# A two-layer attention kernel on one core: one step more between scores, weighing and product, and another order on each queue

## What is computed

```
def gat_layer(x, W, adj):
    Wh, Ws = split(x @ W, 2, axis=-1)
    a = softmax(Wh @ Ws.T, axis=-1) * adj
    return leaky_relu(a @ Wh + x, 0.01)
y = gat_layer(gat_layer(x, W[0], adj), W[1], adj)
out = layernorm(x + y)
```

## Time and profile before

| | us |
|---|---|
| median of 3 runs | 1668.36 |
| the profiled execution | 1670.49 |
| its span, first to last instruction | 1668.1 |
| TensorE matmul busy | 1591.5 (95%) |
| VectorE busy | 1231.2 (74%) |
| GpSimd busy | 872.0 (52%) |
| ScalarE busy | 679.5 (41%) |

### The profile page before, as it was taken

One profiled execution on the slowest core, in us unless ns is written; L12 is line 12 of the kernel. 1 busy time (PEld: TensorE's weight loads), 2 busy tenths in 40 slices (PEclk: granted clock), 3 DMA queues, 4 the chain that ended last, 5 costly groups with the idle time before them and its releaser, 6 DMA issues.

```text
span 1668.1 us, 23318 instructions
## 1 busy us (share of the span) xinstructions
PE 1591.5 (95%) x8104; PEld 1321.9 (79%) x8104; DVE 1231.2 (74%) x1558; ACT 679.5 (41%) x1175; POOL 872.0 (52%) x807
## 2 busy tenths in 40 slices
PE   7899999999999999999889999999999999999996
PEld 6788888887888888887677878887888888888884
DVE  4677777777777777677636787787887888787885
ACT  4434444444444444444333444444434443444442
POOL 0155555555555555555512556555555556555565
PEclk9999999999999999999899999999999999999998
DMA  5267777777667777877915677776778777777774
GB/s 183 81 176 186 190 189 187 185 192 190 185 184 193 184 182 180 206 186 215 249 34 131 176 193 190 192 196 190 179 190 208 191 184 190 196 191 191 195 196 123
DMA packets 167748, 302.57 MB, mean 181 GB/s; under 512 B 39760, under 2 KB 68432, under 8 KB 167504
## 3 DMA queue, kind: packets, MB, share of 16 engines
q1 hardware_dynamic: 105808, 132.75, 32.5%
q0 software_dynamic: 36864, 134.23, 28.0%
q10 hardware_dynamic: 24960, 34.11, 8.5%
HBM read 157.29 MB, written 9.44 MB: 100 GB/s over the span
## 4 chain that ended last, share of the span: by engine, by line
PE 55%; DVE 22%; ACTq 6%; POOL 6%; ACT 5%; issue 3%; DMA 2%; SPq 0%; POOLq 0%
PE banks L474 18%; PE banks L363 10%; PE banks L365 9%; PE banks L364 9%; PE banks L476 8%; DVE neg_max L670 7%; DVE ring L698 7%; ACTq L269 6%; POOL a_lo L795 6%; DVE ring L703 4%; ACT a_hi L588 3%; DMA turned<-ring 1%; ACT ring L571 1%; DVE weight L689 1%; ACT factor L578 1%
## 5 line engine op out<-in xcount | busy, mean ns | idle before, releaser
L795 POOL TENSOR_TENSOR a_lo<-turned,a_hi 128x512 fp32r<-128x512 f32 x512 | 718.5, 1419 | 651.3 <-ACT a_hi L588 651.1
L474 PE MATMUL banks<-wh,a_hi 128*128 128x512 f32 x2048 | 757.7, 408 | 52.1 <-POOL a_lo L795 48.7
L571 ACT ACTIVATE ring<-banks,neg_max 128x1024 f32<-128x1024 f32 x256 | 285.9, 1117 | 818.2 <-DVE neg_max L670 818.2
L476 PE MATMUL banks<-wh,a_lo 128*128 128x256 f32 x2048 | 579.2, 283 | 0.0
L474 PEld LDWEIGHTS banks<-wh,a_hi 128*128 128x128 f32 x2048 | 389.8, 190 | 185.4 <-POOL a_lo L795 81.1
L670 DVE TENSOR_REDUCE neg_max<-banks 128x1 f32<-128x1024 f32 x256 | 311.0, 1215 | 256.7 <-PE banks L365 256.7
L363 PE MATMUL banks<-x_t,q_t 128*128 128x512 f32 x1024 | 405.8, 396 | 4.0 <-DVE x_t L634 2.4
L365 PE MATMUL banks<-x_t,q_t 128*128 128x512 f32 x1024 | 401.7, 392 | 0.0
L364 PE MATMUL banks<-x_t,q_t 128*128 128x512 f32 x1024 | 400.2, 391 | 0.0
L476 PEld LDWEIGHTS banks<-wh,a_lo 128*128 128x128 f32 x2048 | 391.9, 191 | 5.9
L698 DVE SCALAR_TENSOR_TENSOR ring<-ring,weight,load 128x1024 f32<-128x1024 f32 x256 | 376.9, 1472 | 11.5 <-DMA load<-adj 8.8
(11 more groups left out here) (60 smaller groups left out, 668.8 us busy)
## 6 DMA issues: line engine op xcount, KB each, us to landing
load<-adj POOLq DMA_DIRECT2D x256, 512.0 KB, 5.0
turned<-ring SPq DMA_DIRECT2D x1528, 64.0 KB, 4.0
turned<-ring ACTq DMA_DIRECT2D x520, 64.0 KB, 4.0
ring<-x SPq DMA_DIRECT2D x8, 512.0 KB, 5.2
rows<-x SPq DMA_DIRECT2D x32, 128.0 KB, 4.1
x_scratch<-rows SPq DMA_DIRECT2D x32, 128.0 KB, 4.0
rows<-x_scratch SPq DMA_DIRECT2D x32, 128.0 KB, 4.4
first_rows<-x SPq DMA_DIRECT2D x32, 128.0 KB, 3.9
```

The source lines that it names most:

```text
L474: nc.tensor.matmul(psum[:, bank, :], a_hi[:, s, b], wh[:, k].rearrange("p a d -> p (a d)"), start=start, stop=stop, skip_group_check=True)
L476: last = nc.tensor.matmul(psum[:, bank, 0:D], a_lo[:, s, b], wh[:, k, 0], start=False, stop=stop, skip_group_check=True)
L571: nc.scalar.activation(ring[:, i % RING, :].rearrange("p (r b j) -> p b r j", r=2, j=QUAD), psum[:, 2 * (i % 2):2 * (i % 2) + 2, :].rearra ...
L795: nc.gpsimd.tensor_tensor(a_lo[:, j % 2].rearrange("p b (r j) -> p b r j", r=QUADS), as_f32(turned[:, unit % 2, :, b:b + SUB, :]).rearrang ...
```

## The change

- LAG_WEIGH becomes 5, LAG_PRODUCT 8, and `ring` gets a seventh slot; `first_rows` gets one buffer instead of two, with its own load function that waits for the last use.
- Products still all end at the same step of a layer: `products_at` gives step 128 two chunks (120 and 121) and each later step one. Three chunks instead of two are weighed in step 128.
- TensorE: in steps without scores, and up to step 8, products go in front of scores and sides; elsewhere behind, as before. Two of the eight early wh sides of layer 2 move behind the transposes of the late x group (LATE_GROUP, the last 512 rows).
- ScalarE: the factor is made one step later, between the two a_hi of that step. Moves stay behind the exponential; odd chunks have three on ScalarE and five on SP, even ones one and seven (the last four of a layer stay at three and five).
- VectorE: weigh and turn of a chunk that is not among a layer's last four go in front of `row_weights`; finish, normalise and statistics go in front of side splits and of the max.
- GpSimd: the variance power goes in front of the a_lo; in step 128 the adj loads go between the a_lo.
- SP: x groups 11 to 14 are loaded and turned by other tables, one of them between the moves of step 128.

```
-    RING = 6
+    RING = 7
-    LAG_WEIGH = 4
-    LAG_PRODUCT = 7
+    LAG_WEIGH = 5
+    LAG_PRODUCT = 8
...
-                drained = {CHUNKS: [4, 3], CHUNKS + 1: [2], CHUNKS + 2: [1]}
+                drained = {CHUNKS: [5, 4, 3], CHUNKS + 1: [2], CHUNKS + 2: [1]}
...
+        def products_at(step):
+            made = []
+            for of_layer in range(LAYERS):
+                n = step - of_layer * OFFSET
+                if LAG_PRODUCT <= n <= CHUNKS:
+                    made.append(of_layer * CHUNKS + n - LAG_PRODUCT)
+                if CHUNKS <= n <= OFFSET:
+                    made.append(of_layer * CHUNKS + n - LAG_PRODUCT + 1)
+            return made
...
-        X_LOADS = {CHUNKS - 6: [8], CHUNKS: [9, 10, 11, 12], CHUNKS + 1: [13], CHUNKS + 2: [14]}
-        X_TURNS = {CHUNKS: [8], CHUNKS + 1: [9, 10], CHUNKS + 2: [11], CHUNKS + 3: [12], CHUNKS + 4: [13],
-                   CHUNKS + 5: [14]}
+        X_LOADS = {CHUNKS - 6: [8], CHUNKS: [9, 10], CHUNKS + 1: [12], CHUNKS + 2: [13], CHUNKS + 3: [14]}
+        X_LOADS_BETWEEN = {CHUNKS: [11]}
+        X_TURNS = {CHUNKS: [8], CHUNKS + 1: [9, 10], CHUNKS + 3: [11], CHUNKS + 4: [12, 13], CHUNKS + 5: [14]}
...
-            return [("wh", WPAIRS + v) for v in range(EARLY)] if step == LATE_GROUP else []
+            return [("wh", WPAIRS + v) for v in range(EARLY - 2)] if step == LATE_GROUP else []
+        def sides_between(step):
+            return [("wh", WPAIRS + EARLY - 2 + v) for v in range(2)] if step == LATE_GROUP else []
...
-            return chunk_moves[:5 if is_drained(i) else 6]
+            return chunk_moves[:5 if is_drained(i) or i % 2 else 7]
...
+            def load_first_rows(t):
+                if t > TILES:
+                    sp.wait_ge(row_step, row_steps(t - 1) + 3)
+                sp.dma_start(first_rows[:], in_tiles[0][t % TILES]).then_inc(first_loaded, 16)
...
+                if i is None or i % CHUNKS < LAG_PRODUCT:
+                    for k in products_at(step):
+                        product(2 * k)
+                        product(2 * k + 1)
                 if i is not None:
                     scores(i)
                 for side in sides_after(step):
                     make_side(side)
-                if k is not None and not last_product:
-                    product(2 * k)
-                    product(2 * k + 1)
+                if i is not None and i % CHUNKS >= LAG_PRODUCT:
+                    for k in products_at(step):
+                        product(2 * k)
+                        product(2 * k + 1)
...
+                subs = [2 * k + part for k in products_at(step) for part in range(2)]
+                summed = tile_at(step - CPT)
+                for j in subs[:1]:
+                    split_a(j)
+                if summed is not None:
+                    chunk_factors(summed)
+                for j in subs[1:2]:
+                    split_a(j)
+                for j in subs[2:]:
+                    split_a(j)
...
+                for i in weighed_at(step):
+                    if not is_drained(i):
+                        weigh(i)
+                        turn_blocks(i)
                 if ready is not None:
                     row_weights(ready)
                 if late:
                     finish_rows(done)
                 for i in weighed_at(step):
-                    weigh(i)
-                    turn_blocks(i)
+                    if is_drained(i):
+                        weigh(i)
+                        turn_blocks(i)
+                if done is not None and not late:
+                    finish_rows(done)
+                if whole is not None:
+                    normalise_rows(whole)
+                if of_stats is not None:
+                    row_stats(of_stats)
...
+                whole = normalise_at.get(step)
+                if whole is not None:
+                    invert_std(whole)
+                subs = [2 * k + part for k in products_at(step) for part in range(2)]
+                freed = weighed_at(step)
+                if len(freed) > 1:
+                    load_next_adj(freed.pop(0))
+                for j in subs[:2]:
+                    split_a(j)
+                for m in freed[:1]:
+                    load_next_adj(m)
+                for j in subs[2:]:
+                    split_a(j)
+                for m in freed[1:]:
+                    load_next_adj(m)
```

More of the change, by code:

```diff
@@ L143, in gat_layernorm, with row_steps @@
         ROW_STEPS = [1, 5]
+        def row_steps(t):
+            return ROW_STEPS[0] * min(t, TILES) + ROW_STEPS[1] * max(t - TILES, 0)
         def as_f32(ap):
@@ L226, in comes_later @@
             return kind == "q" and n % PAIRS > 0
-        side_order = [("q", 0)] + [s for step in range(STEPS) for s in sides_before(step) + sides_after(step)]
+        side_order = [("q", 0)] + [s for step in range(STEPS) for s in sides_before(step) + sides_between(step) + sides_after(step)]
         side_place = {s: n for n, s in enumerate(side_order)}
@@ L299, in refill_rows, with wait_moved, load_next_x @@
                     load_rows(t + 2)
+            def wait_moved(i):
+                for q in range(2 * (i % 2), 2 * (i % 2) + 2):
+                    sp.wait_ge(moved[i // 2 % 2][q], 64 * (i // 4 + 1))
+            def load_next_x(g):
+                for p in range(2):
+                    sp.wait_ge(rows_stored[p], 16 * 2 * (g - GROUPS + 1))
+                if g in (8, 9):
+                    sp.wait_ge(scores_done, CHUNKS - 2 * CPT * (9 - g))
+                elif g in X_CHUNK:
+                    wait_moved(X_CHUNK[g])
+                else:
+                    sp.wait_ge(xt_done, g - 3)
+                load_x(g)
             def move_blocks(i):
@@ L332, in _ @@
                 if step == LATE_GROUP:
-                    for p in range(2):
-                        sp.wait_ge(rows_stored[p], 16 * (TILES // 2))
-                    load_x(2 * GROUPS - 1)
+                    load_next_x(2 * GROUPS - 1)
                 for g in X_LOADS.get(step, []):
-                    for p in range(2):
-                        sp.wait_ge(rows_stored[p], 16 * 2 * (g - GROUPS + 1))
-                    if g in (8, 9):
-                        sp.wait_ge(scores_done, CHUNKS - 2 * CPT * (9 - g))
-                    elif g in X_CHUNK:
-                        i = X_CHUNK[g]
-                        for q in range(2 * (i % 2), 2 * (i % 2) + 2):
-                            sp.wait_ge(moved[i // 2 % 2][q], 64 * (i // 4 + 1))
-                    else:
-                        sp.wait_ge(xt_done, g - 3)
-                    load_x(g)
+                    load_next_x(g)
                 for i in weighed_at(step):
+                    if is_drained(i) and not is_drained(i - 1):
+                        for g in X_LOADS_BETWEEN.get(step, []):
+                            load_next_x(g)
                     move_blocks(i)
@@ L355, in _ @@
                     refill_rows(stored)
+                took = stats_at.get(step - 1)
+                if took is not None and took + 1 < LAYERS * TILES:
+                    load_first_rows(took + 1)
+                if step == OFFSET:
+                    load_first_rows(TILES)
             for p in range(2):
@@ L499, in _ @@
                     transpose_x(2 * GROUPS - 1)
+                for side in sides_between(step):
+                    make_side(side)
                 for g in x_groups_at(step):
@@ L619, in _ @@
                     split_x(2 * GROUPS - 1)
+                for side in sides_between(step):
+                    split_side(side)
                 for g in x_groups_at(step):
@@ L707, in finish_rows @@
                 acc, y = psum[:, ACC_BANK + p, :], rows[:, p, :]
-                done = ROW_STEPS[0] * min(t, TILES) + ROW_STEPS[1] * max(t - TILES, 0)
+                done = row_steps(t)
                 dve.wait_ge(rows_loaded[p], 16 * (t // 2 + 1))
@@ L776, in _ @@
                         split_side(side)
-                if whole is not None:
-                    normalise_rows(whole)
-                if done is not None and not late:
-                    finish_rows(done)
-                if of_stats is not None:
-                    row_stats(of_stats)
         @block.gpsimd
@@ L808, in _, with load_next_adj @@
                 load_adj(nc.gpsimd, i)
+            def load_next_adj(m):
+                if m + 2 < LAYERS * CHUNKS:
+                    pool.wait_ge(a_done, m + 1)
+                    load_adj(nc.gpsimd, m + 2)
             for step in range(STEPS):
-                k = chunk_at(step - LAG_PRODUCT)
-                if k is not None:
-                    split_a(2 * k)
-                    split_a(2 * k + 1)
-                for m in weighed_at(step):
-                    if m + 2 < LAYERS * CHUNKS:
-                        pool.wait_ge(a_done, m + 1)
-                        load_adj(nc.gpsimd, m + 2)
                 whole = normalise_at.get(step)
```

61 lines of the change are left out of this document (25 added, 36 removed).

## The result

The changed kernel takes **1646.42 us** (median of 4 runs, 1638.25 to 1652.64); the kernel before, on the same chip, 1668.23 (4 runs, 1666.69 to 1671.23). The ratio is 0.9864 (95% interval 0.9819 to 0.9910): 1.4% faster. The forecast was 1640, its own range 1628 to 1651. The profiled execution took 1646.99 us, its span 1643.9, against 1670.49 and 1668.1: 24.2 us of span to account for.

A forecast was written before the change was run, and what follows sets the result against it. TensorE, busy 95% of the span, was taken as the bound. Steady work -28 and +5, boundary -4, late x group -2.4, tail +1 sum to -28.4: 1670.5 to 1642.1, set at 1640 for the median; range 1613 to 1663.

The forecast's parts named there:

- Parts 1 to 4: Steady steps: of 0.83 us stall per tile 0.37 stay, -28 over 60 tiles; layer 2's statistics cost +5.
- Part 1: VectorE's order at tile steps: small operations behind weigh and turn wait for two a_lo, max 0.26 us late.
- Rival B: Steady steps: the stall changes place and 46 of the 50 us remain; 1659, chance 0.18.
- Part 3: ScalarE's moves: a third issue of 0.6 us before a_hi in odd steps; stall charged at 0.37 per tile.
- rival C: Slower: third move delays every odd step's product, 0.52 us each, once its issue costs 1.1 us; 1676, chance 0.10.
- Part 4: Row work ahead of the max: finishing 0, layer 2's statistics +5, GpSimd's power before a_lo 0.
- Part 5: Loads: adj lands before its use two steps on, single first_rows and seventh slot cost nothing; 0, bound +5.
- Part 6: Fills before each layer's first product: one scores more, chain in front one step longer; 0, bounds -3 and +3.
- Part 7: Layer boundary: product 126 before q wins 2.90 us, chunk 123's late unit mostly covered; -4, bounds -10 and +4.
- Part 9: Tail: eighth drained chunk adds 3.75 us, scores end 2.8 earlier, chunk 123's moves late; +1, bounds -3 and +6.
- Rival D: Factor comes too late, the max stays late; only boundary, late x group and tail terms remain; 1663, chance 0.07.
- rival A: Steady steps: the stalls go wholly, all 50 us won; 1613, chance 0.12.

The follow-up runs named there:

- early moves: The changed kernel, but in the first step of each drain ScalarE issues chunk 123's moves ahead of the a_hi of product 121: 1642.77 us, 0.9835.
- drain balanced: The changed kernel with early moves, and chunk 122 with five moves on SP and three on ScalarE, chunk 123 three and five: 1644.20 us, 0.9849.
- the best run: Changed kernel with two ScalarE moves per chunk, q split behind a_hi, drain balanced, chunk 126 late, row work back behind the max: 1620.93 us, 0.9717.
- four and five together: Four: changed kernel with two ScalarE moves per chunk, q split behind a_hi, drain balanced: 1627.06 us. Five: also chunk 126 late: 1628.75 us.
- chunk 126 late: The changed kernel, but in each drain ScalarE's moves of chunk 126 go behind the a_hi of product 124: 1645.68 us, 0.9860.

## Why the prediction was right, and where it wasn't

Forecast and median are 6.4 us apart and the sign is right. On the profiled executions the sum was -28.4 and the span fell by 24.2. The total is nearer than its parts, and that is luck: steady work and fills came out 8 us better than foreseen, the two drains 12 worse. By its parts:

- **Parts 1 to 4, steady work: -23 foreseen, -28.0 measured.** The stalls left are 698.2 + 697.6 - 2 x 685.5 = 24.8 us, against 27 charged. Another 2.8 come from the start: I took 50 us for both layers from layer 1's 24.8, and layer 2 had 28.0, 52.8 in all.
- *Part 1* stands: both small operations meet an a_lo. The tile step shown was 0.04 late, the mean of 58 was 0.24, near the 0.26 I took; but the mean holds steps that were late for TensorE's own stall too. The Trainium skill's rule in "SBUF — State Buffer", section "Who interferes with whom" (a VectorE instruction with two SBUF inputs is kept out by a GpSimd instruction that reads SBUF), is borne out by L727 (mean 723 ns for 164) and L760 (964 for 427). Rival B drew more from it than it does: the operations wait, but mostly inside the slack.
- *Part 3* had the mechanism and too high a price: 0.37 per tile is 11 us a layer; taking the third move away won 4.9, and 7.6 with the row work out of the way. In the median a_hi starts 2.1 us behind the exponential's start with three issues, 1.45 with the old two: 0.65 more, near the 0.6 foreseen and well under the 1.1 from which rival C decides. C's mechanism is real where maxes are late: 69 us a layer.
- *Part 4*: "one operation of the small kind that may wait for the first a_lo: T+4.1, before T+4.36, 0" was wrong. It waits for the second, until T+4.84. I also charged +5 for layer 2's statistics only. Row work cost 1.1 us a layer under the third move (within the spread) and 3.8 without it; the third move alone 7.6, both together 8.7: the prices overlap and don't add. And "GpSimd's power in front of the a_lo has its input a step earlier: 0" fails in the tail, where the statistics come late: 0.9 us (read from the rows; no run took it away).
- *Part 5* holds roughly: weighs wait 13.7 us in all for adj, 8.8 before, and half of it may be hidden.
- *Part 6*, the fills: 0 foreseen, -1.2 and about -1.5 measured, within its bounds.
- **Part 7, the boundary: -4 foreseen, +4.2 measured**, just past the end of its bounds. The step that failed is "surely won is the 2.90 us before q: product 126 goes in front of q". I followed TensorE's order only. On ScalarE, q's split stood between the a_hi of products 126 and 127, so the wait changed place (2.54 us). It costs 2.54 us of waiting and 1.2 of half clock behind it; with q's split behind the a_hi it is 4 us less. The rest lies ahead: products 120 to 123 wait 9.7 us in all for 6.0 before, 3.6 of them in front of product 122, since products 120 and 121 and the x groups did not cover the late start of the unit of chunk 123.
- *Part 8*: -2.4 foreseen. The wait of 2.37 is gone; fill 2 has -4.0 with its own fill.
- **Part 9, the tail: +1 foreseen, +4.7 measured**, inside its bounds (-3 to +6). Chunk 123's delay of 8 us on ScalarE was seen and then taken as partly covered. Products 120 to 123 wait 8.8 us for 4.7 before, and the power adds 0.9. What the forecast left out is SP's queue, whose issues for the same unit end as late (1603.13): "early moves" took away ScalarE's part alone and the tail stayed. With SP relieved as well ("drain balanced") 0.4 to 1.6 us came back, so the runs leave open what makes most of the 4.7.

In sum: steady work 5 us better, fills 2.7, the two drains 12 worse. Rival D and rival A are refuted by the factor's wait (1.4 us) and by the 24.8 us that stay; rival B had 46 staying.

Of the signs named ahead, those for "right" came: the factor's wait gone, 0.41 us of stall per tile, the weigh's mean at 1.31, the waits in odd steps, a longer tail. But so did all three for "wrong": the sum of waits for a_lo hardly changed (46.2 for 48.7), weighs waited for adj (13.7 us), and a product in an odd step stalled 0.92 us behind a punctual max. As tests they were badly chosen: the first adds up drains and steady steps, the others don't say how much.

What stays open: most of what the tail lost; what moves the start of product 126 at the boundary between 40.1 and 47.5 us behind the last max from kernel to kernel; whether the power, put back behind the a_lo, gives its 0.9; and the best run without its late moves of chunk 126, which was not run. By the stretches of four and five together (3.8 us apart) it should lie near 1617, by their ratios near 1620; both are estimates.

## What to carry to other kernels

Slack behind a step is one account. A third issue alone cost 7.6 us a layer, row work alone 3.8, and both together 8.7: so price them together, and remove the largest first, for the smaller one hardly shows while it stands. When work is moved on one engine, walk every in-order queue that feeds it: what stands in front of the next producer there becomes the new wait. In a drain or tail time every queue that feeds the next unit: it starts with the last landing, and relieving one of two equally late queues gave nothing.

## What the hardware showed beyond what was expected

- **An issue is not of constant price.** On ScalarE's queue single issues took 0.51 us, two 1.20, and a third mostly 0.61, but in the step above 1.30 by itself, while SP issued five in 4.43 us beside it. Where that happened TensorE lost 0.9 us. SP's issue of 1.70 us in the tail, where those around it took 0.59, lies beside ScalarE's three.
- **A wait of 2.5 us can cost more than itself.** Windows (us, then PE, PEld, DVE, ACT, POOL busy, granted clock, DMA share, GB/s) behind the wait of 3.58 us before product 122 at the boundary, and around the one before product 127:

```profile
803.80:806.50 2.70, 2.70 (x15) 2.39 (x16) 1.41 (x3) 0.85 (x1) 1.73 (x2) 1.00 1.07 239
830.60:833.10 2.50, 0.03 (x1) 0.00 (x0) 0.69 (x1) 1.63 (x3) 1.24 (x2) 0.96 0.00 0
833.20:835.80 2.60, 2.60 (x8) 2.21 (x9) 0.00 (x0) 0.00 (x0) 1.15 (x1) 0.50 0.00 0
836.50:840.00 3.50, 3.50 (x18) 2.92 (x18) 1.28 (x3) 0.00 (x0) 0.00 (x0) 1.00 0.03 7
```

After 2.54 us idle the granted clock is 0.50 (1.2 GHz): high-part matmuls start 0.64 apart (833.98, 834.62, 835.26), then 0.35 at 1.00 (2.4 GHz). Four distances at 0.64 are 1.2 us more. It doesn't always come: the 3.58 us before product 122 were followed by 1.00, and so were the 2.54 us before product 127 in "chunk 126 late" (835.84). The wait of 2.77 us shown in that run's tail was followed by 0.50 again. Shorter waits of 0.9 us were not followed by it: at 196.35 the next starts 0.45 on. Over all fourteen profiles the four high-part matmuls right behind a wait started 0.6 us apart or more in 1 of 392 cases where it was under 1 us long, in 30 of 104 where it was 2 to 3 us, and in 13 of 14 where it was over 4. So waits that are gathered in one place in a drain can be dearer than the same sum in small ones, and the forecast priced them alike.
